# Wider weight staging in two buffers, and half of an accumulation moved from POOL's DMA queue to VectorE, in a two-layer SSM and mixture-of-experts kernel

## The chip, the cores and the metric

One Trainium2 chip, all 8 cores. Each core runs the same program on one batch element (2048 tokens of width 1024) with all weights; the cores exchange nothing. The metric is device time in microseconds of the slowest core.

## What is computed

Two layers, each x + sequence mixer(xn) + feed-forward(xn) with xn the layer norm of x. The part that the change touches most is the feed-forward of layer 0, with eight low-rank experts over a common pair of weights:

```python
common_w1 = x @ w_gate.T                       # F = 4096
common_w3 = x @ w_up.T
d1 = einsum('enr,efr->enf', einsum('nd,erd->enr', x, A1), B1) * SCALE   # R = 16
d3 = einsum('enr,efr->enf', einsum('nd,erd->enr', x, A3), B3) * SCALE
act = silu(common_w1[None] + d1) * (common_w3[None] + d3)               # 8 experts
out = einsum('ne,enf->nf', weight, act) @ w_down.T
z = einsum('enf,erf->enr', act, A2)
out = out + einsum('ne,enr,edr->nd', weight, z, B2) * SCALE
```

Layer 0's mixer is a gated state-space scan. Layer 1 has a linear recurrence between two 1024 x 1024 products, a shared expert of 1024 hidden columns, and 16 routed experts of 512 hidden columns (w1, w3, w2), all computed densely and weighted.

## The kernel before

Tokens go in four blocks `tb` of 512, held transposed: features on partitions, tokens in the free dimension. Weights are fp32 in HBM and bf16 on the chip.

**Loading weights.** `wload` (line 435) splits what is wider than 512 columns into halves; `wload1` (line 410) takes them in turn through four slots: two buffers `stg` of 1024 fp32 columns, each in two halves. SP issues the DMA into a slot (line 391); a cast to bf16 on ACT (line 426) or, for `w_gate` and `w_up`, on DVE (line 422) frees it. A load into a slot waits for the cast of the load before it in that slot.

**Order.** The program is a list of operations with keys for what they read and write. `_schedule` (line 163) turns it into one fixed order: each operation has a cost from `_COST_TABLE` (line 125), its rank is the longest path of costs from it to the end, and of the operations whose predecessors are already placed, that with the greatest rank comes next. Each engine, SP's queue and POOL's queue too, executes its operations in that order and waits in place for what isn't ready. A DMA on a stream (a semaphore) also follows the one before it on that stream.

**Layer 0's feed-forward** (`l0_ffn`, line 857), for each block:
- Common stage: 32 chunks `fc` of 128 hidden columns; each loads a tile of `w_gate` and one of `w_up` (128 x 1024 each) and does 16 matmuls (lines 874, 889); ACT writes the results as bf16 to PA and PB.
- Expert stage: for each of 8 experts `ex`, 16 pairs `fp` of chunks (1024 columns). PE makes d1 (line 996) into one of two PSUM pairs and d3 (line 1012) into the single pair PP[2]. DVE does t1 = d1 + PA (line 1025) and t3 = d3 + PB (line 1029), ACT does si = silu(t1) (line 1033), POOL does sA, the multiplication by the routing weight `ceb` (line 1038), and DVE does ap = sA * t3 (line 962). Buffers `sss`, `t3s` and `actp` exist twice, by the parity of `fp`, so si(fp+2) waits for ap(fp). PE makes z from the result (line 970). For expert 0, ap writes straight to PC; for the others it writes `actp`, and mx, a DMA of POOL's queue with addition (issued at line 386), adds it to PC: streams `qmx0` and `qmx1` by parity. ap(fp+2) waits for mx(fp) to land.
- Down stage: eight groups of four tiles of `w_down` (cast on ACT), 256 matmuls (line 1093) from PC.

The tiles b1s, b3s (1024 columns) and a2s (512) of an expert are loaded through the same slots.

**Layer 1's routed experts**: eight waves of two experts. A wave loads for each expert eight tiles of w1 and eight of w3 (128 x 512 each, into PA) and four of w2 (128 x 1024, into PB). Then, for each block, SP loads XN (eight DMAs), PE does lines 1371 and 1385 from XN and PA, and the sweep of line 1298 from PB and PC; POOL adds the results to HBM by DMA. There is one XN buffer and one set of weights, so a wave's tiles can be written only after the last block of the wave before has read them.

Of the kernel before, what the change touches and what calls it, by code (L numbers as in the profile page):

```python
# [12 lines left out]
OP = mybir.AluOpType  # L13
# [27 lines left out]
class Prog:  # L41
# [83 lines left out]
_COST_TABLE = (  # L125
    ("d1_", 520), ("d3_", 520), ("z_", 520), ("t1_", 1400), ("t3_", 1400),
    ("si_", 1200), ("sA_", 2500), ("ap_", 750), ("mx_", 2600),
# [95 lines left out]
def K(pool, lo_b, hi_b):  # L223
    return tuple(f"{pool}:{i}" for i in range(lo_b // 512, (hi_b + 511) // 512))
# [84 lines left out]
def build(dbg_internal=False):  # L309
# [13 lines left out]
    with ExitStack() as ctx:  # L323
# [49 lines left out]
        PCb = PC[:, :].bitcast(BF16)  # L373
# [10 lines left out]
        def dma(eng, dst_ap, src_ap, reads, writes, stream, name, accum=False):  # L384
            if accum:
                p.add(eng, (lambda d, s: lambda e: e.dma_start(  # L386
                    out=d, in_=s, accum_op=OP.add))(dst_ap, src_ap),
                    reads=reads, writes=writes, dma=True, stream=stream,
                    name=name)
            else:  # L390
                p.add(eng, (lambda d, s: lambda e: e.dma_start(  # L391
                    out=d, in_=s))(dst_ap, src_ap),
                    reads=reads, writes=writes, dma=True, stream=stream,
                    name=name)
# [12 lines left out]

        stg_ctr = [0]

        def wload1(src_ap, dst_ap, dst_keys, name, ncols, scale_col=None,  # L410
                   scale_keys=(), ceng="S"):
            si4 = stg_ctr[0] % 4
            stg_ctr[0] += 1
            buf, half = si4 // 2, si4 % 2
            lo = half * 512
            assert ncols <= 512
            stk = K(f"stg{buf}", lo * 4, (lo + ncols) * 4)
            dma("sync", stg[buf][:, lo:lo + ncols], src_ap, (), stk,
                f"wst{si4}", "ld_" + name)
            if scale_col is None:  # L420
                if ceng == "V":
                    V((lambda d, s, l, n: lambda e: e.tensor_copy(  # L422
                        d, s[:, l:l + n]))(dst_ap, stg[buf], lo, ncols),
                      stk, dst_keys, "cast_" + name)
                else:
                    S((lambda d, s, l, n: lambda e: e.copy(  # L426
                        d, s[:, l:l + n]))(dst_ap, stg[buf], lo, ncols),
                      stk, dst_keys, "cast_" + name)
            else:
                V((lambda d, s, l, n, sc: lambda e: e.tensor_scalar_mul(  # L430
                    d, s[:, l:l + n], sc))(dst_ap, stg[buf], lo, ncols,
                                           scale_col),
                  stk + scale_keys, dst_keys, "cast_" + name)

        def wload(src_ap, dst_ap, dst_keys, name, ncols, scale_col=None,
                  scale_keys=(), ceng="S"):
            if ncols <= 512:
                wload1(src_ap, dst_ap, dst_keys, name, ncols, scale_col,
                       scale_keys, ceng)
                return  # L440
            for h in range(0, ncols, 512):
                w_ = min(512, ncols - h)
                wload1(src_ap[:, h:h + w_], dst_ap[:, h:h + w_], dst_keys,
                       f"{name}_h{h}", w_, scale_col, scale_keys, ceng)

        for nm, dst, keyn in (("ident", identb[:, :], "identb"),
                              ("onescol", onescol[:, :], "onescol"),
# [409 lines left out]
        def l0_ffn(tb):  # L857
# [43 lines left out]
            for ex in (() if "ffne" in KSKIP else range(E0)):  # L901
# [58 lines left out]
                def flush_a():  # L960
                    fp, par, adst, adk = aq.pop(0)
                    V((lambda adst, par: lambda e: e.tensor_mul(  # L962
                        adst, sss[par][:, :], t3s[par][:, :]))(adst, par),
                      (f"sss{par}", f"t3s{par}"), adk, f"ap_{ex}_{fp}_{tb}")
                    fc0, fc1 = 2 * fp, 2 * fp + 1

                    def mm_z(e, fc0=fc0, fc1=fc1, si=si, adst=adst):
                        inst = None
                        for h, fc in ((0, fc0), (1, fc1)):
                            inst = e.matmul(  # L970
                                PH(6)[0:16, :],
                                a2sb[si][:, fc * 16:fc * 16 + 16],
                                adst[:, h * 512:(h + 1) * 512],
                                start=(fc == 0), stop=(fc == NFC - 1))
                        return inst
                    zq.append((mm_z, (f"a2sb{si}",) + adk, f"z_{ex}_{fp}_{tb}"))
                    if len(zq) > 1:
                        flush_z()
                    if ex > 0:
                        dma("gpsimd", PCb[:, fp * 1024:(fp + 1) * 1024],  # L980
                            adst,
                            adk + PCk(fp * 2048, (fp + 1) * 2048),
                            PCk(fp * 2048, (fp + 1) * 2048),
                            f"qmx{fp % 2}", f"mx_{ex}_{fp}_{tb}", accum=True)

                for fp in range(16):
                    fc0, fc1 = 2 * fp, 2 * fp + 1
# [451 lines left out]
```

How the kernel before makes its waits and increments, by code:

```python
            def body(eng):  # L93
                waited = {}
                for op in prog.ops:
                    if op.eng != eng_name:
                        continue
                    byname = {}
                    for d in prog.deps[op.idx]:
                        if d.token is None:
                            continue
                        sem, val = d.token
                        if val > byname.get(sem, 0):
                            byname[sem] = val
                    for sem in sorted(byname):
                        val = byname[sem]
                        if waited.get(sem, 0) >= val:
                            continue
                        eng.wait_ge(sems[sem], val)
                        waited[sem] = val
                    inst = op.emit(eng)
                    if op.token is not None:
                        assert inst is not None, f"op {op.name} returned None"
                        inst.then_inc(sems[op.token[0]], 16 if op.dma else 1)
                return None
```

## Time and profile before

| | us |
|---|---|
| median of 2 runs | 6379.8 |
| the two runs | 6338.2 and 6421.39 |
| the profiled execution | 6317.83 |
| its span, slowest core (core 7) | 6316.3 |
| spans of the eight cores | 6251.5 to 6316.3 |

The span goes from the first to the last instruction of a core. A group of instructions has its line, engine, operation, tiles and shapes; then busy time, mean length of one in ns, and idle time of the engine ahead of it with what ended it. POOL's and DVE's recorded instructions can overlap by a little, since the next is taken up while the one before it ends.

### The profile page before, as it was taken

How to read it: one execution, taken by the hardware profiler on the slowest of the kernel's cores; microseconds unless marked ns; L12 is line 12 of the kernel's file. 1: busy time of each engine (PE TensorE's matmuls, PEld its weight loads, DVE VectorE, ACT ScalarE, POOL GpSimd, SP SyncE). 2: the span in 40 equal slices, each digit the busy share in tenths (PEclk: the TensorE clock that was granted, in tenths of full speed). 3: DMA queues.
4: the chain of work that ended last, by engine and by line, in shares of the span. 5: the costliest groups of instructions: out<-in, count | busy, mean ns of one | idle time of the engine just before them, and what ended most of it. 6: DMA issues, size and time to landing. Idle time of an engine off the chain costs nothing.

```text
span 6316.3 us, 65028 instructions; the slowest of 8 cores (6251.5 to 6316.3 us)
## 1 busy us (share of the span) xinstructions
PE 4081.2 (65%) x16360; PEld 1430.0 (23%) x16360; DVE 2667.0 (42%) x3432; ACT 1565.0 (25%) x2306; POOL 1847.6 (29%) x1477
## 2 busy tenths in 40 slices
PE   5768755566455574555745566455977877877777
PEld 1223310022100121001200021122433323333333
DVE  1232367833677336872377823411222322222222
ACT  3310123331233323333233331013021121121120
POOL 0001047730477305772067712000101101101101
PEclk8888965579655786557965578777988988888889
DMA  4155734457344572446734463544356466456555
GB/s 115 36 152 132 205 99 98 92 154 213 75 100 91 156 225 71 93 96 158 222 67 90 95 179 108 161 124 129 66 134 124 84 125 127 95 123 117 106 122 73
DMA packets 438717, 762.88 MB, mean 121 GB/s; under 512 B 54993, under 2 KB 110418, under 8 KB 437330
## 3 DMA queue, kind: packets, MB, share of 16 engines
q1 hardware_dynamic: 320082, 523.58, 28.9%
q0 software_dynamic: 118272, 235.14, 21.7%
q8 instruction: 145, 2.38, 0.2%
q14 instruction: 218, 1.79, 0.1%
HBM read 519.75 MB, written 117.64 MB: 101 GB/s over the span
## 4 chain that ended last, share of the span: by engine, by line
PE 39%; DMA 28%; DVE 14%; issue 11%; ACT 4%; SPq 3%; POOL 1%; DVEq 1%; ACTq 0%; POOLq 0%
PE PP L1371 8%; PE PP L1385 7%; DVE scr L1025 5%; PE PP L1298 4%; DMA stg<-wd_s 4%; DMA XN<-xnbd 4%; DMA outT<-osb 4%; DMA stg<-wg_s 3%; DMA stg<-wu_s 3%; DVE t3s L1029 3%; DMA PC<-actp 3%; SPq L391 3%; DVE actp L962 2%; PE PP L815 2%; DMA stg<-w 2%
## 5 line engine op out<-in xcount | busy, mean ns | idle before, releaser
L1038 POOL TENSOR_TENSOR sss<-sss,ceb 128x1024 bf16<-128x1024 bf16 x512 | 1194.8, 2574 | 212.0 <-DMA ceb<-c0d 123.8
L1012 PE MATMUL PP<-xa3s,b3sb 16*128 16x512 bf16 x1024 | 296.3, 568 | 852.7 <-DVE t3s L1029 812.6
L1033 ACT ACTIVATE sss<-scr 128x1024 bf16<-128x1024 bf16 (+1 forms) x512 | 514.8, 1049 | 1178.4 <-DVE actp L962 1028.2
L1371 PE MATMUL PP<-XN,PA 128*128 128x512 bf16 x2048 | 532.1, 407 | 422.0 <-DMA XN<-xnbd 422.0
L386 POOL DMA_DIRECT2D outT<-osb x256 | 223.2, 950 | 1888.6 <-DVE osb L1321 1843.2
L1029 DVE SCALAR_TENSOR_TENSOR t3s<-PP,PB 128x1024 bf16<-128x1024 f32 x512 | 624.5, 1220 | 283.7 <-PE PP L996 186.2
L1398 DVE SCALAR_TENSOR_TENSOR scr<-PP,ceb 128x512 f32<-128x512 f32 x256 | 177.1, 692 | 1133.8 <-PE PP L1385 1132.7
L1025 DVE SCALAR_TENSOR_TENSOR scr<-PP,PA 128x1024 bf16<-128x1024 f32 (+1 forms) x512 | 601.2, 1216 | 120.7 <-PE PP L996 117.3
L1298 PE MATMUL PP<-PC,PB 128*128 128x512 bf16 x2048 | 491.1, 394 | 65.4 <-DVE osb L1321 65.3
L386 POOL DMA_DIRECT2D PC<-actp x448 | 397.7, 1002 | 357.4 <-DVE actp L962 345.2
L1385 PE MATMUL PP<-XN,PA 128*128 128x512 bf16 x2048 | 500.0, 388 | 0.0
L970 PE MATMUL PP<-actp,a2sb 128*16 128x512 bf16 x896 | 434.1, 585 | 49.3 <-DVE actp L962 11.8
L391 POOL DMA_DIRECT2D xa<-osb x96 | 55.1, 575 | 1397.0 <-DVE osb L835 508.1
L1395 ACT ACTIVATE scr<-PP 128x512 bf16<-128x512 f32 x256 | 152.8, 597 | 1162.2 <-PE PP L1371 929.2
L962 DVE TENSOR_TENSOR actp<-sss,t3s 128x1024 bf16<-128x1024 bf16 x448 | 362.7, 844 | 41.4 <-DMA PC<-actp 35.3
L422 DVE CAST SG<-stg 128x512 bf16<-128x512 f32 x512 | 217.0, 427 | 369.8 <-DMA stg<-wu_s 192.6
L1371 PEld LDWEIGHTS PP<-XN,PA 128*128 128x128 bf16 x2048 | 207.6, 102 | 701.1 <-issue 488.3
L874 PE MATMUL PP<-XN,SG 128*128 128x512 bf16 x1024 | 251.9, 391 | 130.4 <-DVE SG L422 119.4
L1012 PEld LDWEIGHTS PP<-xa3s,b3sb 16*128 16x128 bf16 x1024 | 60.6, 98 | 1181.0 <-issue 1181.0
L889 PE MATMUL PP<-XN,SG 128*128 128x512 bf16 x1024 | 253.8, 392 | 83.1 <-DVE SG L422 59.2
L1093 PE MATMUL PP<-PC,SG 128*128 128x512 bf16 x1024 | 246.2, 402 | 78.5 <-ACT SG L426 61.5
L1321 DVE COPY osb<-PP 128x512 f32<-128x512 f32 x256 | 168.9, 686 | 262.4 <-DMA outT<-osb 256.9
(157 smaller groups left out, 4175.8 us busy)
## 6 DMA issues: line engine op xcount, KB each, us to landing
PC<-actp POOLq DMA_DIRECT2D x448, 256.0 KB, 4.1
stg<-w SPq DMA_DIRECT2D x384, 256.0 KB, 4.8
outT<-osb POOLq DMA_DIRECT2D x288, 256.0 KB, 6.1
stg<-wg_s SPq DMA_DIRECT2D x256, 256.0 KB, 4.1
stg<-wu_s SPq DMA_DIRECT2D x256, 256.0 KB, 4.1
stg<-wd_s SPq DMA_DIRECT2D x256, 256.0 KB, 4.0
XN<-xnbd SPq DMA_DIRECT2D x384, 128.0 KB, 4.8
xa<-osb POOLq DMA_DIRECT2D x96, 256.0 KB, 5.3
```

Source lines behind the costliest of these rows:

```text
L386: p.add(eng, (lambda d, s: lambda e: e.dma_start(out=d, in_=s, accum_op=OP.add))(dst_ap, src_ap), reads=reads, writes=writes, dma=True, st ...
L889: inst = e.matmul(PH(6)[:, :], SGb[:, 10240 + si * 1024 + dc * 128: 10240 + si * 1024 + (dc + 1) * 128], XN[:, dc * 512:(dc + 1) * 512], s ...
L962: V((lambda adst, par: lambda e: e.tensor_mul(adst, sss[par][:, :], t3s[par][:, :]))(adst, par), (f"sss{par}", f"t3s{par}"), adk, f"ap_{ex ...
L970: inst = e.matmul(PH(6)[0:16, :], a2sb[si][:, fc * 16:fc * 16 + 16], adst[:, h * 512:(h + 1) * 512], start=(fc == 0), stop=(fc == NFC - 1))
L1012: inst = e.matmul(PP[2][:, h * 512:(h + 1) * 512], b3sb[si][32 * q:32 * q + 16, blk * 128:(blk + 1) * 128], xa3s[si][32 * q:32 * q + 16, : ...
L1025: V((lambda fc0, par, d1p: lambda e: e.scalar_tensor_tensor(scr1[:, :] if par == 0 else scr2[:, :], d1p[:, :], 1.0, PAb[:, fc0 * 512:(fc0 ...
L1029: V((lambda fc0, par: lambda e: e.scalar_tensor_tensor(t3s[par][:, :], PP[2][:, :], 1.0, PBb[:, fc0 * 512:(fc0 + 2) * 512], OP.mult, OP.ad ...
L1033: S((lambda par: lambda e: e.activation(sss[par][:, :], scr1[:, :] if par == 0 else scr2[:, :], AF.Silu))(par), (("scr1",), ("scr2",))[par ...
L1038: G((lambda par, si: lambda e: e.tensor_tensor(sss[par][:, :].rearrange("p (a b) -> p a b", a=2, b=512), sss[par][:, :].rearrange("p (a b) ...
L1298: inst = e.matmul(PH(bank)[:, :], PBb[:, e4 * 4096 + ic * 1024 + oc * 128: e4 * 4096 + ic * 1024 + (oc + 1) * 128], PCb[:, aw:aw + 512], s ...
L1371: inst = e.matmul(PH(b1)[:, :], PAb[:, si * 4096 + dc * 512 + ic * 128: si * 4096 + dc * 512 + (ic + 1) * 128], XN[:, dc * 512:(dc + 1) * ...
L1385: inst = e.matmul(PH(b3)[:, :], PAb[:, 8192 + si * 4096 + dc * 512 + ic * 128: 8192 + si * 4096 + dc * 512 + (ic + 1) * 128], XN[:, dc * 5 ...
```

## The change

Loads: the four slots of 512 columns become two slots of up to 1024 columns (a whole buffer `stg` each); a tile of 1024 columns is one DMA of 512 KB and one cast, and a tile of 512 columns takes a whole slot. Accumulation: for experts 1 to 7 and even `fp`, mx is replaced by mv, an addition on DVE in place in PC (bf16, 128 x 1024, both inputs in SBUF); odd `fp` keep the DMA. The planner's table gets a cost for mv.

```diff
+    ("mv_", 700), ("c1m", 1800), ("c3m", 1800), ("c1e", 800), ("c3e", 800),
...
-            si4 = stg_ctr[0] % 4
+            si = stg_ctr[0] % 2
             stg_ctr[0] += 1
-            buf, half = si4 // 2, si4 % 2
-            lo = half * 512
-            assert ncols <= 512
-            stk = K(f"stg{buf}", lo * 4, (lo + ncols) * 4)
-            dma("sync", stg[buf][:, lo:lo + ncols], src_ap, (), stk,
-                f"wst{si4}", "ld_" + name)
+            stk = K(f"stg{si}", 0, ncols * 4)
+            dma("sync", stg[si][:, 0:ncols], src_ap, (), stk, f"wst{si}",
+                "ld_" + name)
...
-            for h in range(0, ncols, 512):
-                w_ = min(512, ncols - h)
-                wload1(src_ap[:, h:h + w_], dst_ap[:, h:h + w_], dst_keys,
-                       f"{name}_h{h}", w_, scale_col, scale_keys, ceng)
...
                     if ex > 0:
-                        dma("gpsimd", PCb[:, fp * 1024:(fp + 1) * 1024],
-                            adst,
-                            adk + PCk(fp * 2048, (fp + 1) * 2048),
-                            PCk(fp * 2048, (fp + 1) * 2048),
-                            f"qmx{fp % 2}", f"mx_{ex}_{fp}_{tb}", accum=True)
+                        if fp % 2 == 0:
+                            V((lambda fp, adst: lambda e: e.tensor_tensor(
+                                PCb[:, fp * 1024:(fp + 1) * 1024],
+                                PCb[:, fp * 1024:(fp + 1) * 1024],
+                                adst, OP.add))(fp, adst),
+                              adk + PCk(fp * 2048, (fp + 1) * 2048),
+                              PCk(fp * 2048, (fp + 1) * 2048),
+                              f"mv_{ex}_{fp}_{tb}")
+                        else:
+                            dma("gpsimd", PCb[:, fp * 1024:(fp + 1) * 1024],
+                                adst,
+                                adk + PCk(fp * 2048, (fp + 1) * 2048),
+                                PCk(fp * 2048, (fp + 1) * 2048),
+                                f"qmx{fp % 2}", f"mx_{ex}_{fp}_{tb}",
+                                accum=True)
```

## Rows read from the trace of the kernel before

**Rows 1.** The page: busy time of each engine, and the chain that ended last.

```profile
PE 4081.2 (65%) x16360; PEld 1430.0 (23%) x16360; DVE 2667.0 (42%) x3432; ACT 1565.0 (25%) x2306; POOL 1847.6 (29%) x1477
...
PE 39%; DMA 28%; DVE 14%; issue 11%; ACT 4%; SPq 3%; POOL 1%; DVEq 1%; ACTq 0%; POOLq 0%
```

**Rows 2.** Stretches: length, busy PE, PEld, DVE, ACT, POOL; clock, DMA, GB/s.

```profile
1446.00:1611.00 165.00, 121.55 (x512) 47.79 (x512) 54.26 (x125) 34.59 (x64) 1.62 (x3) 0.93 0.76 214
1611.00:2100.00 489.00, 253.67 (x881) 44.21 (x880) 385.50 (x375) 162.91 (x190) 358.94 (x233) 0.56 0.41 84
2122.00:2197.00 75.00, 60.37 (x255) 25.48 (x256) 0.00 (x0) 32.85 (x55) 0.00 (x0) 0.94 0.67 197
```

**Rows 3.** DVE timeline, expert 3, block 1: start, us, operation, [idle].

```profile
1830.56 1.21 DVE L1029 SCALAR_TENSOR_TENSOR t3s<-PP,PB 128x1024 bf16<-128x1024 f32 x1
1832.70 1.22 DVE L1029 SCALAR_TENSOR_TENSOR t3s<-PP,PB 128x1024 bf16<-128x1024 f32 x1 [0.93 <-PE PP L996]
1833.84 2.35 DVE L1025 SCALAR_TENSOR_TENSOR scr<-PP,PA 128x1024 bf16<-128x1024 f32 x2
1836.10 1.73 DVE L962 TENSOR_TENSOR actp<-sss,t3s 128x1024 bf16<-128x1024 bf16 x2
1837.75 1.21 DVE L1029 SCALAR_TENSOR_TENSOR t3s<-PP,PB 128x1024 bf16<-128x1024 f32 x1
```

**Rows 4.** Timeline of POOL in the same stretch.

```profile
1830.64 1.78 POOL L386 DMA_DIRECT2D PC<-actp  x2 [1.17 <-DVE actp L962]
1831.81 4.85 POOL L1038 TENSOR_TENSOR sss<-sss,ceb 128x1024 bf16<-128x1024 bf16 x2
```

**Rows 5.** Timeline of DVE in expert 0 of block 0.

```profile
856.49 1.22 DVE L1029 SCALAR_TENSOR_TENSOR t3s<-PP,PB 128x1024 bf16<-128x1024 f32 x1
...
862.04 1.28 DVE L962 TENSOR_TENSOR PC<-sss,t3s 128x1024 bf16<-128x1024 bf16 x2
863.24 1.22 DVE L1029 SCALAR_TENSOR_TENSOR t3s<-PP,PB 128x1024 bf16<-128x1024 f32 x1
```

**Rows 6.** Timeline of POOL and DVE at the start of block 1.

```profile
1619.65 4.22 POOL L1038 TENSOR_TENSOR sss<-sss,ceb 128x1024 bf16<-128x1024 bf16 x2 [24.17 <-DMA ceb<-c0d]
1621.95 3.07 DVE L962 TENSOR_TENSOR PC<-sss,t3s 128x1024 bf16<-128x1024 bf16 x2 [0.58 <-POOL sss L1038]
```

**Rows 7.** Line 962, ap of expert 0: duration in ns (min/median/max), first, last start.

```profile
L962 DVE TENSOR_TENSOR PC<-sss,t3s x64: 677/684/2471, 847.1 to 3226.3; 128x1024 bf16<-128x1024 bf16 x64
```

**Rows 8.** DMA issues in the common stage: count, KB each, median us to landing.

```profile
stg<-wg_s SPq DMA_DIRECT2D x58, 256.0 KB, 4.1
```

**Rows 9.** Groups of instructions over the whole span.

```profile
L1033 ACT ACTIVATE sss<-scr 128x1024 bf16<-128x1024 bf16 (+1 forms) x512 | 514.8, 1049 | 1178.4 <-DVE actp L962 1028.2 <-DVE PC L962 149.3 <-DVE scr L1025 0.6
...
L386 POOL DMA_DIRECT2D PC<-actp x448 | 397.7, 1002 | 357.4 <-DVE actp L962 345.2 <-issue 8.0 <-PE PP L970 3.8
...
L422 DVE CAST SG<-stg 128x512 bf16<-128x512 f32 x512 | 217.0, 427 | 369.8 <-DMA stg<-wu_s 192.6 <-DMA stg<-wg_s 162.0 <-PE PP L889 5.7
...
L426 ACT CAST SG<-stg 128x512 bf16<-128x512 f32 x256 | 155.6, 616 | 172.3 <-DMA stg<-wd_s 159.2 <-PE PP L1093 9.4
```

**Rows 10.** Tile stg, 5116 to 5141 us: its loads, issue to landing.

```profile
DMA to landing us min/median/max: 2.6/4.1/5.2
```

**Rows 11.** Tile PA, 3984 to 4000 us: loads of 1024 KB, issue to landing.

```profile
DMA to landing us min/median/max: 6.0/6.3/6.8
```

**Rows 12.** PE timeline: waits at the starts of waves 0, 1 and block 1.

```profile
4383.77 3.57 PE L1371 MATMUL PP<-XN,PA 128*128 128x512 bf16 x8 [52.98 <-DMA XN<-xnbd]
...
4645.26 3.57 PE L1371 MATMUL PP<-XN,PA 128*128 128x512 bf16 x8 [22.77 <-DMA XN<-xnbd]
...
4687.90 3.52 PE L1371 MATMUL PP<-XN,PA 128*128 128x512 bf16 x8 [12.39 <-DMA XN<-xnbd]
```

**Rows 13.** SP timeline at a wave border (issues by its queue).

```profile
5071.63 51.45 SPq L391 DMA_DIRECT2D stg<-w  x28
5123.23 3.63 SPq L391 DMA_DIRECT2D XN<-xnbd  x8
```

More of the change, by code:

```diff
@@ L408, in build, with wload @@
         stg_ctr = [0]
-        def wload1(src_ap, dst_ap, dst_keys, name, ncols, scale_col=None,
-                   scale_keys=(), ceng="S"):
-            si4 = stg_ctr[0] % 4
+        def wload(src_ap, dst_ap, dst_keys, name, ncols, scale_col=None,
+                  scale_keys=(), ceng="S"):
+            si = stg_ctr[0] % 2
             stg_ctr[0] += 1
-            buf, half = si4 // 2, si4 % 2
-            lo = half * 512
-            assert ncols <= 512
-            stk = K(f"stg{buf}", lo * 4, (lo + ncols) * 4)
-            dma("sync", stg[buf][:, lo:lo + ncols], src_ap, (), stk,
-                f"wst{si4}", "ld_" + name)
+            stk = K(f"stg{si}", 0, ncols * 4)
+            dma("sync", stg[si][:, 0:ncols], src_ap, (), stk, f"wst{si}",
+                "ld_" + name)
@@ L420, in wload1 @@
             if scale_col is None:
                 if ceng == "V":
-                    V((lambda d, s, l, n: lambda e: e.tensor_copy(
-                        d, s[:, l:l + n]))(dst_ap, stg[buf], lo, ncols),
-                      stk, dst_keys, "cast_" + name)
-                else:
-                    S((lambda d, s, l, n: lambda e: e.copy(
-                        d, s[:, l:l + n]))(dst_ap, stg[buf], lo, ncols),
-                      stk, dst_keys, "cast_" + name)
-            else:
-                V((lambda d, s, l, n, sc: lambda e: e.tensor_scalar_mul(
-                    d, s[:, l:l + n], sc))(dst_ap, stg[buf], lo, ncols,
-                                           scale_col),
+                    V((lambda d, s, n: lambda e: e.tensor_copy(d, s[:, 0:n]))(
+                        dst_ap, stg[si], ncols), stk, dst_keys, "cast_" + name)
+                else:
+                    S((lambda d, s, n: lambda e: e.copy(d, s[:, 0:n]))(
+                        dst_ap, stg[si], ncols), stk, dst_keys, "cast_" + name)
+            else:
+                V((lambda d, s, n, sc: lambda e: e.tensor_scalar_mul(
+                    d, s[:, 0:n], sc))(dst_ap, stg[si], ncols, scale_col),
@@ L433, in wload1 @@
                   stk + scale_keys, dst_keys, "cast_" + name)
[L435 to L440, printed above, removed]
-            for h in range(0, ncols, 512):
-                w_ = min(512, ncols - h)
-                wload1(src_ap[:, h:h + w_], dst_ap[:, h:h + w_], dst_keys,
-                       f"{name}_h{h}", w_, scale_col, scale_keys, ceng)
```

1 row of the table _COST_TABLE is left out of this document.

## The prediction

> **What bounds the kernel now.** I read the page first. No engine is near full: PE 65%, DVE 42%, POOL 29% [rows 1]. The chain that ended last changes its owner often: 39% PE, 28% DMA, 14% DVE [rows 1]. So I read it by stages [rows 2], taking one token block of layer 0 and then the wave borders of layer 1.
>
> In the common-weights stage (lines 865 to 900, 1446 to 1611 us) the DMA engines are 76% busy and move 214 GB/s. In the down-projection (2122 to 2197) it is 197 GB/s at 67%. Loads set the pace of both. In the expert stage (1611 to 2100) DVE has 385.5 us of work in 489, POOL 358.9, and DMA is at 0.41. Four such stages make 1952 us. In the eight expert waves of layer 1 PE works, but stops at each wave's border for its input XN [rows 12].
>
> The steady round of the expert stage handles two `fp`. DVE does t3, [0.93 idle for PE], t3, t1, t1, ap, ap, and begins again 7.19 us later (1830.56 to 1837.75) [rows 3]. Nothing but that 0.93 is idle, so DVE sets the round. POOL starts its two DMAs at 1830.64, its multiplies at 1831.81, and ends at 1836.66 [rows 4]: it has slack. In expert 0, without DMAs, the round takes 6.75 (856.49 to 863.24) [rows 5]. The difference is in ap: the two take 1.73 in [rows 3] and 1.28 in [rows 5].
>
> Why: in [rows 6] DVE starts an ap at 1621.95 while POOL multiplies from 1619.65 to 1623.87. The two ap take 3.07 instead of 1.28. The fastest ap is 0.68 and the slowest 2.47 [rows 7]. An ap that meets a POOL multiply waits to its end and finishes some 0.55 later (1623.87 plus 0.55, then a second of 0.6, gives 1625.02). The t1, which reads PSUM, runs beside POOL's multiply in [rows 3, 4] in 2.35 for two. The operation added here has the form of ap: two bf16 inputs from SBUF.
>
> **The change, part by part.**
>
> *(a) mv in place of half of mx.* It covers 4 blocks x 7 experts x 8 even `fp` = 224 DMAs issued by POOL, 1.0 us of POOL each [rows 9], which become 224 DVE adds. Where do they stand on DVE? The planner ranks by the longest remaining path. Call P the path from ap(fp+2). Then t3(fp+3) has 1400 + P (ap(fp+3) ranks as ap(fp+2) does), mv(fp) has 700 + P, and t1(fp+4) has 1200 + 1400 + 2500 + P - 4450 = P + 650 (a round of the chain si, sA, ap is 1200 + 2500 + 750). So mv goes behind the second t3 and ahead of t1, not into the 0.93 gap ahead of t3.
>
> Now one round, timed from the end of the first ap: it starts at 1836.10 - 7.19 = 1828.91 and takes 1.73 less 0.6 for the free second one, so it ends at about 1830.03. A lone multiply takes 4.22 / 2 = 2.1 [rows 6], so those that end at 1836.66 really run from 2.4 to 4.5 and on to 6.6. With one DMA issue less ahead of them I put them 0.3 earlier: 2.1 to 4.25, and on to 6.35. DVE ends its second t3 at 3.89. mv meets the first multiply, waits to 4.25, ends at 4.8. The second multiply then waits 0.6 and ends at 6.9, just as the first ap starts at 7.0, which is thereby free and takes 0.68 instead of 1.12. The round is 7.68: +0.5. Bounds: mv isn't blocked at all, 0.60 - 0.44 = +0.16; mv loses to the second multiply also, below. I take +0.46 x 224 = **+103**. The odd mx stays, and with it the wait of ap for a landed DMA at expert borders; from the 489 - 7 x 57.5 - 54 = 32 us at eight borders I allow **-10**.
>
> The Trainium skill says, in "SBUF — State Buffer", section "Who interferes with whom", that a DVE instruction with two SBUF inputs and a GpSimd instruction that reads SBUF exclude each other for a whole instruction. The trace agrees (3.07 instead of 1.28 us). It speaks against the change: POOL was relieved, but the new work goes to the engine that sets the round and through the shared port.
>
> *(b) Four slots of 512 columns become two of 1024.* For loads of 1024 columns as many bytes are in flight, but a slot now stays closed through a longer load and cast. A slot's round now is load 4.1 + cast 0.43 + issue about 0.15 = 4.7 us [rows 8, 9], four slots, so 1 MB per 4.7. What lands 512 KB? No row. One 256 KB load nearly alone takes 2.6 [rows 10]; 1024 KB took at least 6.0 [rows 11]; so 1.13 per added 256 KB and 3.7 for a lone 512 KB; as 256 KB goes from 2.6 to 4.1 under traffic, I put 512 KB at 4.6 (bounds 3.7 and 2 x 4.1 = 8.2, nearer the first, since the bytes in flight don't grow). The DVE cast of 1024 lies between 0.43 and 0.86; I take 0.75. Two slots: 4.6 + 0.9 = 5.5 per 1 MB, 17% slower. A common-weights stage of some 150 us gets +20, as part of it hides behind PE (121.6 busy of 165): 4 x 20 = **+80**. In the down-projection the cast is on ACT: 0.62 for 512 [rows 9], 1.05 for 1024 columns, as the silu of that width takes [rows 9]: round 4.1 + 0.75 = 4.85 before, 4.6 + 1.3 = 5.9 after, +21% of 75 us, less the eight tiles loaded ahead: 4 x 12 = **+48**. The other bursts (winT, woT twice, bw, cw, ws1 to ws3: 72 tiles of 0.5 MB, 36 rounds of 4.7 us = 170 us) get 17%, **+30**, taken as wholly exposed.
>
> *(c) w1 and w3 have 512 columns, so for them the depth falls from four to two.* There are 256 loads. At a wave border PE waits 22.77 us for XN, and 12.39 us at the next block [rows 12]; the borders after it look alike. XN isn't late by itself: SP issues 28 weight loads from 5071.63 on and reaches XN only at 5123.23 [rows 13], since each load waits for a cast to free its slot. Eight of the 28 belong to the wave's second expert. With two slots, that expert has eight loads in each slot's chain, not four, so the planner puts about twelve ahead of XN. Before, eight loads in two rounds of some 4.8 us; after, twelve in six rounds of 4.0 (a load between 2.6 and 4.1 [rows 10], 3.2 with two in flight, + 0.75): +14 us. The first expert's loads, which today end 3 us before the sweep does, need seven rounds rather than three and a half and come 5 us late. +19 at each of 7 borders = +133, and +15 at the first wave (52.98 us of wait [rows 12]): **+148**. Bounds: +8 a border (loads at 2.6) and +30.
>
> Sum: 103 - 10 + 80 + 48 + 30 + 148 = +399. On the profiled execution's 6317.8 us this is 6717, say 6720. The two runs shown have a median of 6379.8, 1% above that execution, which the range has to hold too.
>
> What hides nothing: fewer instructions on ACT, SP and POOL (half the casts and issues) lie on engines that wait for data. If the cover of PE in the common stage were gone, the full 17% would cost 6 us more per block.
>
> **Rivals.**
>
> 1. *Large transfers pay for themselves.* A 512 KB load lands in 3.7 under traffic also; the round is 3.7 + 0.9 = 4.6, and (b) costs nothing; in (c) two loads in flight land in 2.6, +8 a border. Sum 103 - 10 + 60 = +153: 6470, within 2%. For it: the bytes per DMA double with the same number in flight. Against it: DMA is at 0.76 already, so queueing and not issue fills the 4.1. The Trainium skill, "DMA: Bandwidth & Descriptors", section "Bandwidth", advises batching towards 1 MiB; no run here shows that yet.
>
> 2. *POOL keeps the port.* Its second multiply follows the first at once, recorded 2.1 later; if it takes the port before the waiting mv, mv ends at 6.35 + 0.55 = 6.9, t1, t1, ap follow, and the round is 9.8: +2.6 x 224 = 582 instead of 103. 7196. It decides if POOL releases the port between its instructions or not; no DVE operation of that form crosses such a border in this trace. I think the one that already waits wins.
>
> 3. *Faster.* DVE adds fall into the 0.93 gap, if mv stands ahead of the second t3. The round is then that of expert 0: 6.75, -0.44 x 224 = -99; with rival 1's loads costing nothing and earlier border DMAs -40: about 6180. The point is the rank: 700 + P against 1400 + P speaks against it.
>
> 4. *Nothing to be seen.* The unblocked bound (+36), loads as in rival 1 and slack at the borders: 6317.8 + 36 + 40 = 6390.
>
> **Numbers.** Forecast 0.68, rival 1 0.12, rival 2 0.10, rival 3 0.05, rival 4 0.05. A difference under 2% (128 us) can't be told from none here. Faster 0.05, same 0.12 + 0.05, of which some of rival 1 lands above: 0.15; slower 0.80. The forecast's own range is 6540 to 6920 (load landing 4.1 to 5.2, border +12 to +27). The range down to 6470 takes in rival 1 and up to 7020 part of what lies between the forecast and rival 2; outside are rivals 2 to 4, 0.20 together.
>
> **What would show it.** mv directly behind the second t3 with a mean near 1.0 us (0.68: unblocked; over 2.5: rival 2); a round of about 7.7; expert stage about 513 us instead of 489; stg loads of 512 KB landing in about 4.6; common stage 185 us instead of 165; the wait for XN at a wave border about 40 us instead of 22. I am wrong if the expert stage shrinks, or if weight loads keep 215 GB/s.

## The result, and the profile after

The changed kernel takes 6615.35 us (median of 11 runs, 6561.86 to 6712.5) beside 6422.47 of the kernel before (10 runs, 6304.3 to 6480.93): a ratio of 1.0403, 95% interval 1.0351 to 1.0454. It is slower. In some executions of either kernel the cores of one die, or of both, show a lower granted clock and the time is longer; the medians here include such executions and the ratios leave them out, so a ratio isn't the quotient of the medians beside it. The profiled execution took 6594.73 us, 277 more than the 6317.83 of before; the spans of its cores are 6528.8 to 6593.2.

The page of the changed kernel, busy time and chain, against [rows 1]: DVE has 166 us more busy time, POOL 195 less, and neither says where the 277 us went.

```profile
PE 4210.0 (64%) x16360; PEld 1452.0 (22%) x16360; DVE 2833.0 (43%) x3392; ACT 1509.6 (23%) x1981; POOL 1652.6 (25%) x1253
...
PE 37%; DMA 26%; DVE 14%; issue 13%; ACT 4%; POOL 3%; SPq 3%; DVEq 1%; ACTq 0%; POOLq 0%
```

The stretches of token block 1 on core 7 (common, expert, down), with the columns of [rows 2]: 178 us instead of 165, 544 for the expert stage, 80 instead of 75. The 544 must not be set beside the 489 of [rows 2]: that stretch ends with the last d1, at 2100, and the first down matmul comes at 2122.5 only. Counted up to there as here, the stage before took 511 us. Loads fall from 214 to 198 GB/s in the first and from 197 to 176 in the last.

```profile
1545.00:1723.00 178.00, 124.32 (x512) 47.17 (x510) 44.73 (x65) 34.51 (x63) 1.62 (x3) 0.93 0.66 198
1723.00:2267.00 544.00, 281.89 (x897) 49.98 (x896) 444.41 (x440) 167.99 (x183) 323.18 (x185) 0.56 0.25 57
2267.00:2347.00 80.00, 64.72 (x256) 26.56 (x256) 0.00 (x0) 27.07 (x26) 0.00 (x0) 0.88 0.56 176
```

The timeline of DVE in a steady round, expert 3 of block 1 (columns as in [rows 3]). A round goes from 1933.84 to 1941.88: 8.04 us instead of 7.19. The new addition, mv (L964), stands between the two t1 (L1018).

```profile
1933.84 1.23 DVE L1022 SCALAR_TENSOR_TENSOR t3s<-PP,PB 128x1024 bf16<-128x1024 f32 x1
1935.92 1.23 DVE L1022 SCALAR_TENSOR_TENSOR t3s<-PP,PB 128x1024 bf16<-128x1024 f32 x1 [0.86 <-PE PP L1005]
1937.07 1.22 DVE L1018 SCALAR_TENSOR_TENSOR scr<-PP,PA 128x1024 f32<-128x1024 f32 x1
1938.20 1.24 DVE L964 TENSOR_TENSOR PC<-PC,actp 128x1024 bf16<-128x1024 bf16 x1
1939.37 1.21 DVE L1018 SCALAR_TENSOR_TENSOR scr<-PP,PA 128x1024 bf16<-128x1024 f32 x1
1940.50 1.28 DVE L945 TENSOR_TENSOR actp<-sss,t3s 128x1024 bf16<-128x1024 bf16 x2
1941.88 1.23 DVE L1022 SCALAR_TENSOR_TENSOR t3s<-PP,PB 128x1024 bf16<-128x1024 f32 x1
```

The timeline of POOL beside it, against [rows 4]: its two multiplies end at 1938.88, and mv, begun at 1938.20, ends 0.56 after that, at 1939.44.

```profile
1934.43 4.45 POOL L1031 TENSOR_TENSOR sss<-sss,ceb 128x1024 bf16<-128x1024 bf16 x2
```

The round can be accounted for from the start of one operation to the start of the next. mv adds 1.17 (1938.20 to 1939.37). The two ap (L945) take 1.38 (1940.50 to 1941.88) where [rows 3] has 1.65 (1836.10 to 1837.75), since the multiplies have ended by then: -0.27. The stretch from t3 to t3 is 0.06 shorter (2.08 against 2.14). Together +0.84. Not every round is like this one: in the mean of the eight cores 36 of the 224 mv take under 0.8 us and 30 over 1.35. On the profiled core, mv's durations in ns (min/median/max) are:

```profile
L964 DVE TENSOR_TENSOR PC<-PC,actp x224: 681/1242/2689, 972.0 to 3934.0; 128x1024 bf16<-128x1024 bf16 x112
```

The loads of 1024 columns, in the same stretch as the common stage above (columns of [rows 8]); then the DVE cast of that width:

```profile
stg<-wg_s SPq DMA_DIRECT2D x29, 512.0 KB, 4.2
stg<-wu_s SPq DMA_DIRECT2D x29, 512.0 KB, 4.3
...
L419 DVE CAST SG<-stg x60: 683/694/696, 1551.6 to 1713.5; 128x1024 bf16<-128x1024 f32 x60
```

A wave border of layer 1 in the timeline of SP, against [rows 13]: 22 weight loads take 56.71 us, and only then are the eight XN issued. Twelve of the second expert's loads stand ahead of XN in the planner's order, where the kernel before has eight.

```profile
5136.66 56.71 SPq L391 DMA_DIRECT2D stg<-w  x22
5193.83 3.70 SPq L391 DMA_DIRECT2D XN<-xnbd  x8
```

The timeline of PE at the same border and at the next two blocks, against [rows 12]: 37.44 us of wait for XN instead of 22.77, but 8.65 and 2.43 at the blocks behind it. Before the third, PE does 32 matmuls of the sweep (L1291).

```profile
5202.67 3.57 PE L1364 MATMUL PP<-XN,PA 128*128 128x512 bf16 x8 [37.44 <-DMA XN<-xnbd]
...
5241.36 3.57 PE L1364 MATMUL PP<-XN,PA 128*128 128x512 bf16 x8 [8.65 <-DMA XN<-xnbd]
...
5277.58 7.07 PE L1291 MATMUL PP<-PC,PB 128*128 128x512 bf16 x32
5287.07 1.89 PE L1364 MATMUL PP<-XN,PA 128*128 128x512 bf16 x8 [2.43 <-DMA XN<-xnbd]
```

**One table for all kernels.** The stages below were timed alike in each profiled execution, from first matmuls: common from the first of line 874 to the first d1; expert from there to the first down matmul; down from its first to its last matmul; middle from the last down matmul to the first expert wave; waves from there to the end. Each figure is a median over the eight cores (for `three_slots` over cores 0 to 3), and the first three are sums over the four blocks. The last columns are PE's wait for XN in us: at the first wave, and the mean over the seven later waves at blocks 0, 1, 2, 3.

| kernel | common | expert | down | middle | waves | span | XN, first wave | XN, blocks 0/1/2/3 |
|---|---|---|---|---|---|---|---|---|
| before | 632 | 2032 | 291 | 641 | 1924 | 6265 | 53.0 | 23.1/13.2/6.5/6.4 |
| after | 700 | 2186 | 322 | 667 | 1909 | 6541 | 78.7 | 35.7/7.8/2.3/2.0 |
| mv_only | 620 | 2184 | 291 | 631 | 1917 | 6390 | 52.6 | 23.2/12.9/6.6/6.5 |
| mv_behind_ap | 627 | 2066 | 284 | 634 | 1918 | 6285 | 51.9 | 22.7/12.9/6.8/6.7 |
| mv_ahead_t1 | 628 | 2334 | 288 | 638 | 1923 | 6570 | 52.8 | 23.3/12.9/6.8/6.5 |
| loads_only | 694 | 2019 | 324 | 666 | 1903 | 6374 | 78.6 | 35.2/8.6/1.9/1.9 |
| halves_512 | 696 | 2178 | 328 | 650 | 1902 | 6511 | 61.1 | 24.9/10.2/6.6/6.7 |
| sweep_early | 696 | 2184 | 325 | 667 | 1956 | 6595 | 79.6 | 35.5/7.9/4.8/4.6 |
| sweep_late | 625 | 2028 | 293 | 636 | 1848 | 6211 | 52.4 | 23.1/13.1/2.6/2.1 |
| xn_whole | 634 | 2031 | 291 | 630 | 1880 | 6231 | 51.6 | 22.8/9.7/6.2/5.8 |
| best | 630 | 2028 | 294 | 629 | 1789 | 6132 | 51.6 | 7.3/9.7/2.3/2.2 |
| three_slots | 556 | 2024 | 256 | 632 | 1946 | 6201 | 56.8 | 24.6/10.1/6.5/5.9 |
| combined_r5 | 553 | 2026 | 255 | 630 | 1786 | 6009 | 55.3 | 1.6/9.0/2.2/2.0 |

A stage that an edit doesn't touch differs by up to some 13 us between executions (expert: 2019 to 2032). The waves and the span of `three_slots` can't be compared with the others: on core 0 the granted clock from 5000 to 5600 us was 0.77, beside 0.88 in the kernel before; up to 3600 us the two had the same.

From before to after: common +68, expert +154, down +31, middle +26 (all of it the wait for XN at the first wave, 53.0 to 78.7), waves -15; the remaining 12 of the 276 lie outside these stages. In the waves, PE's waits for XN fall by 22 us in all (369 to 347), but PE has 33 us of a wait that the kernel before doesn't have, some 5 us for ACT's `scr` in block 3 of most waves.

### The profile page after: what moved, and what is told of

Read it like the earlier page. It is cut to its first block, busy times and chain, and to the rows that moved or that the text cites. A ratio compares the mean times of both kernels' runs of the same rounds, so it can differ in the third digit from the quotient of the medians.

```text
span 6593.2 us, 60915 instructions; the slowest of 8 cores (6528.8 to 6593.2 us)
## 1 busy us (share of the span) xinstructions
PE 4210.0 (64%) x16360; PEld 1452.0 (22%) x16360; DVE 2833.0 (43%) x3392; ACT 1509.6 (23%) x1981; POOL 1652.6 (25%) x1253
## 4 chain that ended last, share of the span: by engine, by line
PE 37%; DMA 26%; DVE 14%; issue 13%; ACT 4%; POOL 3%; SPq 3%; DVEq 1%; ACTq 0%; POOLq 0%
PE PP L1364 7%; PE PP L1378 7%; DMA stg<-wg_s 5%; DMA outT<-osb 4%; DVE actp L945 4%; DMA stg<-wd_s 3%; PE PP L1291 3%; DMA stg<-w 3%; DVE t3s L1022 3%; POOL sss L1031 3%; DMA XN<-xnbd 3%; DMA stg<-wu_s 2%; SPq L391 2%; DVE scr L1018 2%; PE PP L683 2%
## 5 line engine op out<-in xcount | busy, mean ns | idle before, releaser
L1031 POOL TENSOR_TENSOR sss<-sss,ceb 128x1024 bf16<-128x1024 bf16 x512 | 1130.0, 2312 | 218.9 <-DMA ceb<-c0d 121.3
L1026 ACT ACTIVATE sss<-scr 128x1024 bf16<-128x1024 f32 (+1 forms) x512 | 513.5, 1048 | 1354.9 <-DVE actp L945 1198.6
L1018 DVE SCALAR_TENSOR_TENSOR scr<-PP,PA 128x1024 f32<-128x1024 f32 (+1 forms) x512 | 618.7, 1215 | 111.5 <-PE PP L989 111.2
L1291 PE MATMUL PP<-PC,PB 128*128 128x512 bf16 x2048 | 471.5, 384 | 37.4 <-DVE osb L1314 37.2
L419 DVE CAST SG<-stg 128x1024 bf16<-128x1024 f32 x256 | 177.1, 693 | 461.8 <-DMA stg<-wg_s 207.7
L386 POOL DMA_DIRECT2D PC<-actp x224 | 198.6, 886 | 691.9 <-DVE actp L945 666.3
L989 PE MATMUL PP<-xa1s,b1sb 16*128 16x512 bf16 x1024 | 294.6, 580 | 31.2 <-ACT b1sb L422 28.5
```

Of the source, the lines that this page charges most:

```text
L386: p.add(eng, (lambda d, s: lambda e: e.dma_start(out=d, in_=s, accum_op=OP.add))(dst_ap, src_ap), reads=reads, writes=writes, dma=True, st ...
L989: inst = e.matmul(d1p[:, h * 512:(h + 1) * 512], b1sb[si][32 * q:32 * q + 16, blk * 128:(blk + 1) * 128], xa1s[si][32 * q:32 * q + 16, :], ...
L1018: V((lambda fc0, par, d1p: lambda e: e.scalar_tensor_tensor(scr1[:, :] if par == 0 else scr2[:, :], d1p[:, :], 1.0, PAb[:, fc0 * 512:(fc0 ...
L1026: S((lambda par: lambda e: e.activation(sss[par][:, :], scr1[:, :] if par == 0 else scr2[:, :], AF.Silu))(par), (("scr1",), ("scr2",))[par ...
L1031: G((lambda par, si: lambda e: e.tensor_tensor(sss[par][:, :].rearrange("p (a b) -> p a b", a=2, b=512), sss[par][:, :].rearrange("p (a b) ...
L1291: inst = e.matmul(PH(bank)[:, :], PBb[:, e4 * 4096 + ic * 1024 + oc * 128: e4 * 4096 + ic * 1024 + (oc + 1) * 128], PCb[:, aw:aw + 512], s ...
```

## The experiments

The theory after the first comparison: the two parts cost independently; mv costs its place in DVE's order; the loads cost because two slots are too few; and the waves gain because the planner's order changed. The rivals: the parts work against each other in DMA or on DVE; wide DMAs are slow in themselves; the waves gain from the wider loads.

### Each part alone

`mv_only` is the kernel before with mv in place of half of mx and its planner cost; `loads_only` is the changed kernel with every mx back, the reverse of this edit. Its diff against the changed kernel:

```diff
-                        if fp % 2 == 0:
-                            V((lambda fp, adst: lambda e: e.tensor_tensor(
...
+                        dma("gpsimd", PCb[:, fp * 1024:(fp + 1) * 1024],
+                            adst, ...
```

> The kernel before with the accumulation part of the change alone; loads keep four slots. Theory A (the two parts add): the expert stage grows as in the changed kernel, from about 509 to 542 to 554 us a block, the waves and the load-bound stages stay as before; sum about +150 us, ratio 1.024. Rival (the parts interact, the add costs only beside the wider loads): expert stage under 525 us, ratio under 1.01.

> The kernel before with the staging part alone; all mx stay DMAs. Theory A: common stage +17 us a block, down stage +7 us, expert stage unchanged at about 509, waves -38 to +13 us in total; sum about +100 us, ratio 1.015. If the planner's new order of the sweeps comes from the loads alone, the waits for XN at blocks 1 to 3 of a wave are near 8, 2 and 1 us as in the changed kernel and not 13, 6 and 8. Rival: the waves' change comes from the accumulation part; then those waits stay at 13, 6 and 8.

`mv_only`: 6493.56 us median, ratio 1.0201 (1.0145 to 1.0257). `loads_only`: 6444.89, ratio 1.0206 (1.0136 to 1.0277). The two excesses add up to 4.07%, and the whole change has 4.03%: no interaction is needed. The table gives mv the expert stage (+152) and nothing else, and the loads the common stage (+62), down (+33), middle (+25) and waves (-21).

### The place of mv

`mv_behind_ap` is `mv_only` with a lower rank for mv, so that it comes behind both ap of its round:

```diff
+        if o.name.startswith("mv_"):
+            x, f, b = o.name[3:].split("_")
+            prio[i] = min(prio[at[f"ap_{x}_{f}_{b}"]],
+                          prio[at[f"ap_{x}_{int(f) + 1}_{b}"]]) - 1
```

> mv_only with mv ranked directly behind the two ap of its round, where POOL isn't yet multiplying. Theory P (mv costs 1.24 and not 0.68 us because it waits for POOL's multiply, and stands in DVE's way): mv takes 0.68, the round falls from 8.05 to about 7.3 us, the expert stage to about 512 us a block, ratio to before near 1.00. Rival Q (any 0.68 us or more on DVE delays the chain ap, si, sA by as much wherever it stands): round about 7.9, ratio near 1.02.

The timeline of DVE in `mv_behind_ap` (mv is L987):

```profile
1886.21 1.28 DVE L968 TENSOR_TENSOR actp<-sss,t3s 128x1024 bf16<-128x1024 bf16 x2
1887.60 0.69 DVE L987 TENSOR_TENSOR PC<-PC,actp 128x1024 bf16<-128x1024 bf16 x1
...
1893.69 1.28 DVE L968 TENSOR_TENSOR actp<-sss,t3s 128x1024 bf16<-128x1024 bf16 x2
```

Behind ap, mv takes 0.69 us, because POOL's next multiply starts at 1888.20 only. The round is 7.48 us and the expert stage 2066 instead of 2184; the ratio to the kernel before is 1.0096 (1.0025 to 1.0168). So of mv's +152 us some 118 go with the place at which it meets the multiply. The other 34 are what is left when it doesn't: mv still takes 0.61 from its start to the next (1887.60 to 1888.21), and with one DMA issue less on POOL the two ap and the stretch between the t3 get about 0.3 back. So even at the better place the relieved POOL gives back less than mv costs.

`mv_ahead_t1` is `mv_only` with mv ahead of both t1, the place that the prediction had given it:

```diff
+            j = [at.get(f"t1_{x}_{int(f) + k}_{b}") for k in (4, 5)]
+            if None not in j:
+                prio[i] = max(prio[j[0]], prio[j[1]]) + 1
```

> mv_only with mv ranked ahead of both t1, the place that the prediction gave it (in the changed kernel it stands between them). The prediction's sum said: mv meets POOL's first multiply, wins the port at its end, takes about 1.0 us, the round is 7.7, the expert stage about 525 us a block. Rival 2 of the prediction: POOL keeps the port through its second multiply, mv takes near 3 us, round 9.8, stage over 570. Third: mv takes 1.0 and the second multiply is pushed back so far that ap waits again; round 8.0, stage about 545 as now.

The timelines of DVE (mv is L988) and then of POOL:

```profile
1904.14 1.28 DVE L969 TENSOR_TENSOR actp<-sss,t3s 128x1024 bf16<-128x1024 bf16 x2
...
1908.75 2.37 DVE L988 TENSOR_TENSOR PC<-PC,actp 128x1024 bf16<-128x1024 bf16 x1
...
1913.31 1.27 DVE L969 TENSOR_TENSOR actp<-sss,t3s 128x1024 bf16<-128x1024 bf16 x2
```

```profile
1906.12 4.45 POOL L1055 TENSOR_TENSOR sss<-sss,ceb 128x1024 bf16<-128x1024 bf16 x2
```

The round is 9.17 us (1904.14 to 1913.31), the expert stage 2334, the median of five runs 6805.61 (6584.14 to 6851.86; no ratio was obtained). mv comes to DVE at 1908.75, when the first multiply is over (half of 4.45 after 1906.12 is 1908.3) and the second has begun; it waits the second one out (1910.57) and ends 0.55 later, at 1911.12. The same instruction takes 0.69, 1.24 or 2.37 us by its place.

The Trainium skill, "SBUF — State Buffer", section "Who interferes with whom", calls the port pair that the two engines share an exclusive lock, and says that the order of issue decides which of them is blocked. The three places agree: 0.69 when no multiply is running, the rest of a multiply plus 0.55 when one is.

### The loads

`three_slots` is `loads_only` with a third buffer `stg`; to make room, the tiles a1Tb and a3Tb share the memory of two tiles that are not in use at the time:

```diff
-        stg = [sb(f"stg{i}", [128, 1024]) for i in range(2)]
+        stg = [sb(f"stg{i}", [128, 1024]) for i in range(3)]
...
-            si = stg_ctr[0] % 2
+            si = stg_ctr[0] % 3
```

> loads_only (mx all DMAs, 1024-column loads) with a third buffer of 1024 columns; a1T and a3T reuse the space of two phase-1 weights. Theory D (a slot is closed during its longer load and cast, so depth is what fell): common stage back from 175 to about 155 to 160, down stage from 81 to about 73, border wait from 35 to under 28; ratio to before near 1.00. Rival T (the wider DMA itself moves fewer bytes per us): common stays over 170 and down near 80.

The stretch of the common stage, block 1, core 0 (columns of [rows 2]):

```profile
1388.00:1525.00 137.00, 117.45 (x506) 49.65 (x504) 44.38 (x65) 34.99 (x63) 1.91 (x3) 0.93 0.78 251
```

With three slots the loads run at 251 GB/s, and PE is busy 117.5 of 137 us. In the same stage of the same core it was 196 GB/s after the change and 221 before it (198 and 214 on core 7). The four common stages take 556 us (before 632, two slots 694), down 256 (291, 324). The ratio to the kernel before is 0.9745 (0.9613 to 0.9878). So loads of 512 KB are not slow in themselves: three of them in flight beat the four small ones, and what cost time in the change is having two. Three slots hold 1.5 MB, though, where the kernel before and the change hold 1 MB, so this run doesn't tell which of more bytes in flight or fewer instructions gives the gain over before. In the waves the waits for XN are about those of before, 6.5 and 5.9 us at blocks 2 and 3 again; the 1946 us were taken at the lower clock and show no loss.

The Trainium skill, "DMA: Bandwidth & Descriptors", section "Bandwidth", advises to batch DMAs to 1 MiB or more. By that rule alone the change should have gained. Here, in the common stage of core 0, 512 KB loads through two slots lost 25 GB/s, and the same loads through three gained 30.

`halves_512` is the changed kernel with four half slots again for tiles of 512 columns (w1, w3), two whole ones for the rest:

```diff
+            if ncols == 512:
+                n4 = half_ctr[0] % 4
+                half_ctr[0] += 1
+                lo = (n4 % 2) * 512
```

> The changed kernel; tiles of 512 columns (w1, w3, a2s) take half a buffer again, in four slots; 1024-column tiles stay whole in two slots. Theory C (the border's length comes from w1 and w3 having two slots, and through the slot chain also the planner's order of the sweeps): border wait back from 35.7 to 23, wait of the first wave from 79 toward 55, blocks 2 and 3 back to 6.5, waves near 1924; common and down stages stay at 177 and 81. Total within 20 us of the changed kernel. Rival (the wide w2 tiles lengthen the border): border wait stays over 30.

The wait at the wave border goes back to 24.9 us (before 23.1, after 35.7) and that of the first wave to 61.1 (53.0, 78.7), so the lost depth for w1 and w3 is the cause of the longer border. But the waves as a whole gain only 7 us, 1902 instead of 1909, because the waits at blocks 2 and 3 come back too (6.6 and 6.7). The median is 6654.71 (6523.43 to 6719.9); no ratio was obtained, the profiled span is 30 us shorter than after's.

### The order of the waves

The sweep of line 1298 is eight chunks of eight matmuls for each block, placed by rank among the matmuls of the blocks. In the kernel before, PE's timeline has two chunks (16 matmuls) ahead of a block that waits:

```profile
5214.75 3.62 PE L1298 MATMUL PP<-PC,PB 128*128 128x512 bf16 x16
5224.46 3.19 PE L1371 MATMUL PP<-XN,PA 128*128 128x512 bf16 x8 [6.09 <-DMA XN<-xnbd]
```

After the change it is four chunks, 7.07 us of work that covers the reload of XN (the last fence on PE above). Two runs move the order alone. `sweep_early` is the changed kernel with the sweeps as early as in the kernel before; `sweep_late` is the kernel before with the second half of each sweep held back:

```diff
+            if int(b) < 3 and int(oc) >= 4:
+                x = 2 * int(wv) + 1
+                prio[i] = min(prio[i], prio[at[f"eh3_{x}_3_{int(b) + 1}"]] - 1)
```

> The changed kernel; only the sweep chunks of blocks 0 to 2 are ranked where the kernel before has them (two chunks at a time through the next block, two at its end). Loads and mv as in the changed kernel. Theory S (order alone hides XN at blocks 2 and 3): the waits there return from 2.3 and 2.0 to about 6.5 each, the border stays at 35, block 1 at 8; the waves grow from 1909 to about 1980 us, ratio to before near 1.05. Rival (with two slots fewer loads compete with XN, so XN lands sooner whatever the order): waits at blocks 2 and 3 stay near 2, waves near 1909.

> The kernel before; only the rank of the last four sweep chunks of blocks 0 to 2 of a wave is lowered, so that they stand behind the next block's last matmuls, as in the changed kernel. Theory S (the changed kernel's waves gain back their longer borders by this order): waits for XN at blocks 2 and 3 fall from 6 to 8 us to 2 or less, the waves shrink by 60 to 110 us, ratio 0.985 to 0.99. Rival: the waits only move (to the sweep's evictions or the border), ratio 1.00.

`sweep_early`: the waves take 47 us more than after the change (1956), the waits at blocks 2 and 3 are 4.8 and 4.6 instead of 2.3 and 2.0 (expected: 6.5), ratio to before 1.0523 (1.0404 to 1.0643). `sweep_late`: 76 us less (1848), waits 2.6 and 2.1 instead of 6.5 and 6.4, median 6337.39 (6246.2 to 6447.97) beside 6367.18 of before; no ratio was obtained. So the order by itself, with the loads of before, gives the whole gain at blocks 2 and 3. Taking it away from the changed kernel takes back some 5 of the 8.6 us a wave; what keeps the rest is not shown.

Block 1 gained also (13.2 to 7.8), and SP's timeline of the kernel before shows a reason: the eighth XN stands behind two weight loads. After the change (second fence) the eight stand together.

```profile
5160.89 3.17 SPq L391 DMA_DIRECT2D XN<-xnbd  x7
5164.21 0.87 SPq L391 DMA_DIRECT2D stg<-w  x2
5165.18 0.40 SPq L391 DMA_DIRECT2D XN<-xnbd  x1
```

```profile
5232.85 3.64 SPq L391 DMA_DIRECT2D XN<-xnbd  x8
```

`xn_whole` is the kernel before with that one load ranked as its neighbour:

```diff
+        if "_xnb2_" in o.name:
+            prio[i] = prio[at[o.name.replace("_xnb2_", "_xnb3_")]]
```

> The kernel before, only the eighth XN load of a block ranked with the other seven, so that no weight load stands ahead of it. Theory: the wait at block 1 of a wave falls from 13.2 to 8 to 10, as in the changed kernel, which is the rest of what its waves gained; waves -25 to -40 us, ratio 0.995. Rival: the wait stays, since the other seven land no sooner.

Block 1's wait is 9.7 instead of 13.2 and the waves take 1880 instead of 1924; median 6388.68 (6243.99 to 6398.95) beside 6342.62, no ratio. The 3.5 us at seven blocks are 25 of the 44 us. Over all blocks of all waves PE's waits for XN fall by 38 us (369 to 331), a few tenths at the other blocks and some 8 us in the first wave.

### Versions that beat both kernels

`best` is the kernel before with `sweep_late`, `xn_whole`, and XN of a wave's first block ranked just ahead of the first expert's third w2 tile, so that the second expert's loads stand behind it:

```diff
+        if o.name[0] == "w" and "_xnb" in o.name and o.name.endswith("_0"):
+            x = 2 * int(o.name[1])
+            prio[i] = prio[at[f"ld_w2_{x}_2_h0"]] + 1
```

> The kernel before with three changes of rank: sweep_late; all eight XN loads of a block together (today two weight loads stand ahead of the eighth); XN of a wave's first block ahead of the second half of the first expert's w2. Theory: block 1's wait falls from 13 to 8, blocks 2 and 3 to 2.5, the border's from 23 to 10 to 18 with part of it given back by the second expert's weights; waves from 1924 to about 1750 to 1800, ratio 0.97 to 0.98. Rival: at the border the weights take what XN gives; waves as in sweep_late less 40, ratio 0.98 to 0.985.

The waves take 1789 us, 135 less: ratio 0.9762 (0.963 to 0.9895), with no change to a single instruction. The border waits 7.3 us for XN instead of 23.1, but this third rank change gives little: `sweep_late` and `xn_whole` alone have 76 and 44 of the 135. PE's waits for XN fall by 206 us over the waves, and 75 of them come back as a wait for ACT 32 matmuls into block 0 of each wave. The last fences of `combined_r5` below show the same wait and its reason.

`combined` is `three_slots` with the ranks of `best`; it was run twice.

> three_slots with the three rank changes of best. If the gains lie in different stages they add: common 139, down 65, expert 506, waves 1780 to 1810; span near 6060, ratio near 0.95. Rival (faster loads meet the waves' new order and cancel): waves over 1850, ratio 0.965.

> The same kernel as combined, timed in five rounds, since the first timing gave no interval. The theory in which depth and order add: common stage about 140 a block, down about 64, the waves about 1790 by an order with the sweep chunks late and XN first, and a ratio of 0.95 to 0.96 to the kernel before (cores 0 to 3 of the first profile, 6028, against 6265 of before is 0.962). The rival, in which the two gains overlap (both feed the same queue at the block border), gives no more than the better of the two alone, 0.975.

The first time gave no ratio (6053.17 to 6358.32 us, before 6342.62). The second: 6088.79 us (6031.0 to 6272.48) beside 6339.99, ratio 0.9637 (0.958 to 0.9694). Common 553 and down 255 are those of `three_slots`, waves 1786 those of `best`: the two gains add. PE's timeline at blocks 1 and 2 of a wave shows waits that were 13.2 and 6.5 in the mean:

```profile
5199.78 3.57 PE L1368 MATMUL PP<-XN,PA 128*128 128x512 bf16 x8 [8.69 <-DMA XN<-xnbd]
5244.88 1.89 PE L1368 MATMUL PP<-XN,PA 128*128 128x512 bf16 x8 [1.46 <-DMA XN<-xnbd]
```

The border of the wave before that one, in the timelines of SP, of ACT and then of PE. XN goes out ahead of the second expert's loads, but ACT still has the casts of these loads ahead of the silu that PE waits for (L1392).

```profile
4905.67 5.28 SPq L405 DMA_DIRECT2D XN<-xnbd  x8
4911.10 27.66 SPq L405 DMA_DIRECT2D stg<-w  x15
4938.92 0.33 SPq L405 DMA_DIRECT2D ceb<-c1d  x1
```

```profile
4939.55 0.62 ACT L436 CAST PA<-stg 128x512 bf16<-128x512 f32 x1 [0.60 <-DMA stg<-w]
4941.04 0.62 ACT L436 CAST PA<-stg 128x512 bf16<-128x512 f32 x1 [0.88 <-DMA stg<-w]
4941.57 0.59 ACT L1392 ACTIVATE scr<-PP 128x512 bf16<-128x512 f32 x1
```

```profile
4942.41 3.57 PE L1368 MATMUL PP<-XN,PA 128*128 128x512 bf16 x8 [15.48 <-ACT scr L1392]
```

Such waits come to 110 us over the waves. `ceb`, the routing weights, is issued behind the same loads, so DVE would have stood until then too. Bringing the silus and `ceb` forward as well is the next step; no run tries it.

## Why the prediction was right, and where it was not

The direction and the range held: 6720 was said (6470 to 7020), 6615 came. But against the profiled execution the sum was +399 and +277 came, and the terms missed by more than the sum did. The expert stage cost 61 us more than said, all else together some 185 less, so part of the agreement is luck.

| term | predicted | measured |
|---|---|---|
| mv, 224 rounds | +103 (0.46 a round) | 0.84 in the steady round |
| expert stage in all | +93 | +154 |
| common stage | +80 | +68 |
| down stage | +48 | +31 |
| other bursts | +30 | +3 ahead of block 0, none in the middle |
| first wave's XN | +15 | +26 |
| seven borders | +133 (19 each) | +88 (12.6 each) |
| blocks 1 to 3 of the waves | 0 | -98 (7 x (5.4 + 4.2 + 4.4)) |

**mv's place failed.** The step "mv(fp) has 700 + P, and t1(fp+4) has P + 650, so mv goes ahead of t1" compared mv only with the t1 of its own parity. The sum for that one is right, mv ranks 50 above t1(fp+4). But in the changed kernel the odd chain still ends in mx, with 2600 of cost behind its last ap, and t1(fp+5) ranks 330 above mv: DVE has t1(odd), mv, t1(even). The mechanism (mv waits to the end of a multiply, then 0.55) was right, and met the second multiply instead of the first: 1.17 us instead of 0.91. `mv_ahead_t1` shows that the predicted place would not have given the predicted round either: 9.17 instead of 7.68, since the multiplies start early enough for mv to fall into the second.

**The relief of ap was mis-sized.** The prediction took 0.44 off, the difference of two durations. From start to start the two ap take 1.65 before and 1.38 after: 0.27. With 1.17 and 0.06 that is +0.84. Times 224 it would be 188, and the stage got 154. Some 36 of the 224 mv weren't blocked (under 0.8 us), which makes up part of the difference; the rest I didn't split. The prediction's +93 also started from too short a stage: its 489 us leave out the last 22 (see the result), and four stages are 2032 us, not 1952.

**The loads: right in mechanism, somewhat too dear.** A 512 KB load lands in 4.2 to 4.3 us (said 4.6; rival 1 had 3.7), the DVE cast takes 0.69 (0.75). From one load to the next in the same slot, over the four common stages, the median was 4.7 us before, as said, and 5.25 after (said 5.5). So the slot's round grew by 12% and the stage by 11% (632 to 700), not 17%; +20 a block became +17. At the start and the end of a stage a tile that has landed waits longer for its cast (up to 17 us in block 1 of core 7, 0.1 in the middle), so in both kernels the stage is longer than its 32 rounds.

**The waves failed by omission.** The border was seen (said 40 us of wait; 37.44 and 33.79 in two waves on core 7, 35.7 in the mean), and so was its cause, twelve loads of the second expert ahead of XN; its price was 12.6 us, not 19. What wasn't: the edit of the load function changes the cost of every path through a weight tile, so the planner also reorders PE's and SP's work elsewhere. That gave 98 us of waits for XN back at blocks 1 to 3. "The borders after it look alike" was taken as a constant of the kernel, and it was a result of the ranks.

**The rivals.** Rival 1 (large transfers pay): not here, 214 to 198 GB/s; with a third slot, and half as many bytes again in flight, yes. Rival 2 (POOL keeps the port): not in the changed kernel. In the steady round of `mv_ahead_t1` mv comes when the second multiply has begun, so its 2.37 us don't decide it; 40 of its other mv show it, with 3.14 us (last section). Rival 3 (faster): its place, the gap of 0.86 us ahead of the second t3, was never taken, and wasn't tried. Rival 4: nothing for it.

## What to carry over

Where a planner orders the program, an edit to one operation's cost or shape is an edit to the order of all: list the new order on every queue before pricing anything, and don't assume that a wait elsewhere stays as it was. Price a staging change by the time in which a slot is closed and by the number of slots, for each width that goes through it. Equal bytes in flight aren't enough: two slots of 512 KB hold what four of 256 KB hold, and lost, since a slot's round (load, cast, issue) was 12% longer. And when one load is moved ahead in one queue, look at what the other queues still have in the old order. Work that shares a port with another engine has no duration of its own: look up what the other engine does at the very place where it will stand.

## What the runs showed of the chip that I had not expected

Who gets the port between two multiplies of POOL that follow one another goes both ways. I looked at each DVE operation of two bf16 inputs that started during the first multiply of a pair, on all eight cores. In the changed kernel all 22, in `mv_only` all 10 and in `mv_behind_ap` all 32 ended 0.55 us after the first multiply: DVE got in between. In `mv_ahead_t1` 26 did so, and 40 waited for the second multiply too. Both kinds, in the timeline of `mv_ahead_t1`, core 0, DVE:

```profile
1140.39 3.14 DVE L988 TENSOR_TENSOR PC<-PC,actp 128x1024 bf16<-128x1024 bf16 x1
...
2099.91 1.72 DVE L988 TENSOR_TENSOR PC<-PC,actp 128x1024 bf16<-128x1024 bf16 x1
```

and POOL:

```profile
1138.46 4.53 POOL L1055 TENSOR_TENSOR sss<-sss,ceb 128x1024 bf16<-128x1024 bf16 x2
...
2098.95 4.68 POOL L1055 TENSOR_TENSOR sss<-sss,ceb 128x1024 bf16<-128x1024 bf16 x2 [2.61 <-DMA ceb<-c0d]
```

In the 40 the record of the second multiply begins 0.34 us before the first one's ends, and mv started 0.15 to 0.20 before that record; in all others the two records overlap by 0.03 only. How early mv started doesn't separate them: 1.12 us of duration came of a start 0.57 us before the first multiply's end, 3.14 of one some 0.50 before it. Nor does the order of the recorded starts, since mv's is the earlier in all. It looks as if a second multiply that has been taken up already keeps the port, but no run tests it, and it stays open.
